# Layer 0 of a two-layer graph network on Trainium2: where a finished block's norm, flip and layer 1 products stand

## What is computed

```python
h = jnp.maximum(_layernorm(x), 0.0)
x = x + L0(h)   # feat = h @ W[type]; e = leaky_relu(el + er); softmax of e over the edges
                # of one target; sum over them of alpha * feat[src]; + h_bias
h = jnp.maximum(_layernorm(x), 0.0)
x = x + L1(h)   # h_all = h @ (8 relation matrices); sum over edges of h_all[src, type];
                # + h @ loop_w + h_bias + h; gelu; layer norm with gamma, beta
```

## Time and profile before

| | us |
|---|---|
| median of 3 runs | 2796.43 (2791.49 to 2800.01) |
| profiled execution, its span | 3432.1 |
| of it: until the first softmax (L1370) | 267.9 |
| the loop, first to last L1370 | 1673.9 |
| last L1370 to the first gather of layer 1 | 92.2 |
| first to last gather of layer 1 | 1361.7 |
| behind it | 36.4 |
| busy in the span: PE 1960.6, DVE 1538.5, ACT 667.0, POOL 2024.5 | |

### The profile page before, as it was taken

One profiled execution on the slowest core, in us unless ns is written; L12 is line 12 of the kernel. 1 busy time (PEld: TensorE's weight loads), 2 busy tenths in 40 slices (PEclk: granted clock), 3 DMA queues, 4 the chain that ended last, 5 costly groups with the idle time before them and its releaser, 6 DMA issues.

```text
span 3432.1 us, 26416 instructions
## 1 busy us (share of the span) xinstructions
PE 1960.6 (57%) x8092; PEld 1402.3 (41%) x8092; DVE 1538.5 (45%) x3220; ACT 667.0 (19%) x1202; POOL 2024.5 (59%) x2138
## 2 busy tenths in 40 slices
PE   7873536666665666566575772544544434554445
PEld 6772324444443444344453441333333322333334
DVE  6763546555655555455565540222332322323324
ACT  4423122333332323233323120000000000000001
POOL 6736555655555555555655527666666666666663
PEclk9985667788787878787787895666666766666667
DMA  8455334444443444444443333233333333333332
GB/s 229 158 189 174 103 98 119 128 132 130 131 136 111 138 122 128 120 129 120 135 133 112 97 129 104 84 93 93 98 98 92 97 92 100 96 95 98 97 92 70
DMA packets 168505, 403.12 MB, mean 117 GB/s; under 512 B 49741, under 2 KB 75820, under 8 KB 160682
## 3 DMA queue, kind: packets, MB, share of 16 engines
q0 software_dynamic: 95312, 261.58, 28.1%
q1 hardware_dynamic: 73050, 139.85, 11.8%
HBM read 325.41 MB, written 75.86 MB: 117 GB/s over the span
## 4 chain that ended last, share of the span: by engine, by line
PE 36%; another core or an unknown queue 28%; DVE 19%; issue 13%; ACT 1%; DVEq 1%; POOL 1%; DMA 0%; ACTq 0%; POOLq 0%
PE PB L1844 20%; PE PB L1955 6%; DVE ACC L1328 5%; DVE Z L1356 5%; PE PB L1796 4%; PE PB L1919 3%; DVE OHZ L1538 2%; DVE ERM L1337 1%; DVE OHZ L1346 1%; PE PB L1960 1%; POOL Z L841 1%; PE PB L1903 1%; DVEq L1315 0%; PE PB L1958 0%
## 5 line engine op out<-in xcount | busy, mean ns | idle before, releaser
L841 POOL DMA_INDIRECT Z<-tab,KI x1963 | 1868.2, 952 | 1260.0 <-issue 560.2
L1844 PE MATMUL PB<-Z,OHZ 128*128 128x260 f32 (+1 forms) x3926 | 1190.0, 459 | 808.0 <-issue 522.9
L1844 PEld LDWEIGHTS PB<-Z,OHZ 128*128 128x128 f32 x3926 | 861.5, 229 | 1085.3 <-issue 668.6
L1328 DVE TENSOR_TENSOR ACC<-ACC,PB 128x260 f32 (+1 forms) x997 | 421.4, 423 | 1493.4 <-remote 1031.1
L1919 PE MATMUL PB<-pick,ERM 128*128 128x16 f32 (+1 forms) x504 | 113.3, 375 | 476.2 <-DVE ERM L1337 440.4
L1919 PEld LDWEIGHTS PB<-pick,ERM 128*128 128x128 f32 (+1 forms) x504 | 109.9, 330 | 489.9 <-DVE ERM L1337 452.8
L1356 DVE TENSOR_TENSOR Z<-Z,PB 128x2048 f32<-128x2048 f32 (+1 forms) x125 | 283.9, 2271 | 0.0
L1955 PE MATMUL PB<-w,ht 128*128 128x512 f32 x480 | 271.5, 729 | 1.8 <-ACT ht L1714 1.8
L1776 ACT ACTIVATE ACC<-ACC 128x256 f32<-128x256 f32 x30 | 10.4, 406 | 857.2 <-DVE ACC L1328 857.2
L1955 PEld LDWEIGHTS PB<-w,ht 128*128 128x128 f32 x480 | 112.2, 241 | 139.0 <-issue 136.4
L1796 PE MATMUL PB<-wh,hx 128*128 128x424 f32 (+1 forms) x500 | 152.2, 375 | 20.7 <-DVE hx L933 15.7
(11 more groups left out here) (333 smaller groups left out, 1498.4 us busy)
## 6 DMA issues: line engine op xcount, KB each, us to landing
OHZ<-dlt SPq DMA_DIRECT2D x31, 1024.0 KB
Z<-tab,KI POOLq DMA_INDIRECT x1963
tab<-st SPq DMA_DIRECT2D x120, 256.0 KB
tab<-Z SPq DMA_DIRECT2D x24, 1040.0 KB, 4.3
TD<-typ SPq DMA_DIRECT2D x31, 256.0 KB
tab<-Z SPq DMA_DIRECT2D x5, 1024.0 KB, 8.1
xn<-xb SPq DMA_DIRECT2D x30, 128.0 KB
X<-xn SPq DMA_DIRECT2D x6, 640.0 KB
```

The source lines that it names most:

```text
L841: pool.indirect_dma_start(to, None, tab, at).then_inc(d_fe[g % 2][part(g, k) * layer], 16)
L1328: dv.tensor_tensor(a, a, bank(done + i)[:, 0:width], ALU.add).wait_op(*previous, "sem-ge").then_inc(*o.of(s_add))
L1844: last = pe.matmul(p, OH[:, slot, k + i, :], rows_, start=(i == 0), stop=(i == n - 1))
```

## The change

- `finish(r)` becomes a generator in two parts. Up to `ve` it runs behind `rescale` of its group, ahead of the second `scale_rows`; `rs` and `nmr` follow behind the adds of the first three pairs.
- On PE flip, products and own product of block r stand in group r+4, between the fourth pair and `select`. The quarters go to PB0, PB6, PB7 and PB1, the own product to PB0, the flip to PB1, each with a wait for the add that frees it (`s_add`). The fifth pair waits for `s_own`.
- On ACT `normed` and `move_flipped` stand behind the two exponentials of the group; the moves of the quarters and the own product stand behind `turned` and ahead of `stage` of the next turn.
- SP stores the block's table rows in the same group.
- After the loop the block in hand (27) is flipped in the midst of the last pairs, blocks 28 and 29 have a tile of their own each for the flipped rows (`HTL`), the transposes of the index tables stand between the products, and the three own products follow all quarters. The cast of `KI` is DVE's.

PE at the end of a group in the middle of the loop, before: from the first half of the next group's scores (L1903) to the softmax's transpose (L1986).

The core of the diff (PE's part and the sync engine's are told above and by the rows):

```diff
@@ finish(r) on DVE
-                norm_scale(r, r + 1, FIN + r)
+                dv.tensor_scalar(ve[:, r:r + 1], mv[:, r:r + 1, 1], 1e-5, None, ALU.add).then_inc(*o.of(s_ve))
+                yield
+                dv.wait_ge(s_sd, no)
+                dv.reciprocal(rs[:, r:r + 1], sd[:, r:r + 1]).then_inc(*o.of())
...
+                norm = finish(finished_in(g)) if finished_in(g) >= 0 else iter(())
+                next(norm, None)
                 for c in range(8, n, 8):
                     scale_rows(g, c)
...
+                    if c == 8:
+                        next(norm, None)
...
-                if finished_in(g) >= 0:
-                    finish(finished_in(g))
...
+            for i in range(2):
+                dv.wait_ge(s_pt, KT + i + 1)
+                dv.tensor_copy(KI[:, 512 * i:512 * i + 512], PB[6 + i][:, :]).then_inc(*o.of(s_ki))
@@ ACT's loop
                 if g + 1 < NG:
                     turned(g + 1)
+                r = finished_in(g - 1)
+                if r >= 0:
+                    for j in range(4):
+                        move_quarter(r, j)
+                    move_own(r)
+                if g + 1 < NG:
                     stage(g + 1)
...
                 ac.activation(EX[0:R, :], ZR[0:R, :], ACT.Exp).then_inc(*o.of(s_xr))
+                r = finished_in(g)
+                if r >= 0:
+                    normed(r)
+                    move_flipped(r)
@@ PE, flip and products
+                if r < LATE:
+                    pe.wait_ge(s_add, pair_no(r + 4, 1))
+                elif r > LATE:
                     pe.wait_ge(s_ev, moved(r - 1, 3))
...
+                    if r < LATE and j < 3:
+                        pe.wait_ge(s_add, pair_no(r + 4, j + 2))
...
+            block_products(LATE)
+            flip_block(LATE + 1)
             pe.wait_ge(s_loc, 4)
-            pe.wait_ge(s_own, last)
...
             pe.wait_ge(s_add, NPAIR)
+            turn_back(lambda t: ERM[:, 128 * t:128 * t + 128], (PB[6], PB[7]))
+            block_products(LATE + 1)
+            flip_block(LATE + 2)
+            turn_back(lambda t: TD[:, t, :], (PB[0], PB[1]))
+            block_products(LATE + 2)
+            for r in range(LATE, NB):
+                own_product_of(r)
```

More of the change, by code:

```diff
@@ L721, in _ @@
                 sp.dma_start(rows[:, i, :], t.rearrange("(o n) -> o n", o=1).to_broadcast([128, D])).then_inc(d_rows, 16)
[L722 to L730, removed]
+            store_block(LATE)
+            load_block(LATE + 2)
+            store_block(LATE + 1)
+            store_table(LATE)
+            store_block(LATE + 2)
+            store_table(LATE + 1)
+            store_table(LATE + 2)
             for i in range(2):
@@ L1457, in finish @@
                 s = r % 2
+                no = FIN + r
                 a = ACC[:, ROW0 * r:ROW0 * r + D].rearrange("p (h d) -> p h d", h=4)
@@ L1526, in _ @@
                     load_places(g + 1)
-                if finished_in(g) >= 0:
-                    finish(finished_in(g))
             for q in range(added_in_turn(NG - 1), GROUPS[NG - 1][1] // 2):
                 add(pair_no(NG - 1, q), ROW0, 0)
-            finish(NB - 2)
-            finish(NB - 1)
+            for r in range(LATE + 1, NB):
+                for _ in finish(r):
+                    pass
+            for i in range(2):
+                dv.wait_ge(s_pt, KT + i + 1)
+                dv.tensor_copy(KI[:, 512 * i:512 * i + 512], PB[6 + i][:, :]).then_inc(*o.of(s_ki))
             def onehot(g):
@@ L1695, in move_quarter @@
                     ac.wait_ge(d_st[j], 16 * r)
[L1696 removed]
+                ac.activation(ST1[:, j, :], quarter_bank(r, j)[:, :], ACT.Copy).then_inc(*o.of(s_ev))
             def move_own(r):
[L1700 to L1701 removed]
+                ac.wait_ge(s_mm, own_product(r))
+                ac.activation(ACC[:, ROW0 * r:ROW0 * r + D], own_bank(r)[:, 0:D], ACT.Copy).then_inc(*o.of(s_own))
             def normed(r):
@@ L1923, in late @@
             def late(g, a, b):
+                r = finished_in(g) if g >= 0 else -1
+                if a == 4 and 0 <= r < LATE:
+                    pe.wait_ge(s_own, r + 1)
                 for q in range(a, min(b, GROUPS[g][1] // 2)) if g >= 0 else ():
@@ L2007, in _ @@
                 late(g, 3, 4)
+                r = finished_in(g)
+                if 0 <= r < LATE:
+                    flip_block(r)
+                    block_products(r)
+                    own_product_of(r)
                 if g + 1 < NG:
                     select(g + 1)
[L2010 to L2031 removed]
+            late(NG - 1, 4, 8)
+            flip_block(LATE)
+            late(NG - 1, 8, 16)
+            block_products(LATE)
+            flip_block(LATE + 1)
+            pe.wait_ge(s_loc, 4)
+            pe.wait_ge(s_add, NPAIR)
+            turn_back(lambda t: ERM[:, 128 * t:128 * t + 128], (PB[6], PB[7]))
[3 more added lines that the diff above has]
+            block_products(LATE + 2)
+            for r in range(LATE, NB):
+                own_product_of(r)
+            pe.wait_ge(s_ki, 2)
+            pe.wait_ge(s_kt, KT + 2)
             pe.wait_ge(s_own, NB)
[L2033 removed]
             for g in range(len(GROUPS1)):
```

129 lines of the change are left out of this document (51 added, 78 removed).

## The result

| | us |
|---|---|
| before, median of 7 runs | 2796.43 (2791.49 to 2800.01) |
| after, median of 7 runs | 2808.54 (2801.67 to 2809.48) |
| ratio | 1.0039, 95% interval 1.0029 to 1.0049 |
| profiled execution of after, its span | 2807.0 |

The change makes the kernel 12 us slower; 33 us faster was forecast. The span of this record is that of the runs, so recording costs nothing here. The record of before came from an execution of 3432 us. The first set of experiments shows that the same kernel can take that long without a profile too; why it does stays open. All rows of "before" in this part are of that second record.

A forecast was written before the change was run, and what follows sets the result against it. The prediction took a chain of waits through DVE and PE to bound each group, with POOL second. Gains of 22 us in the loop and 11 behind it made 33: 2796.4 - 33 = 2763 us, range 2731 to 2804.

The forecast's parts named there:

- The two make 710, near the 636: Recorded span against median: late semaphores (560 us) and longer layer 1 gathers (150) were laid to recording, explaining 635.7 us.
- So the chain goes from 39.4 to 38.7: DVE and PE's scan-to-scan chain in the loop: 38.5 to 38.7 us, gain 0.8 a group, 22 us in 27 groups.
- POOL holds the group: Rival, chance 0.22: POOL's 32 gathers hold a group at 40.1 us, only the tail is won, 2785 us.
- the 0.30 between gathers may be the record's: POOL's gathers: the argument against POOL as bound, that the 0.30 us between gathers may come from recording.
- The middle of the group: Scan to `nmr` 20.7 us, then products 9.4 and own product 2.2 ahead of `select`; EV to scan 1.2.
- The clock: PE's moved products: 7.1 us at the high clock, 9.4 as recorded, 14.0 all at the low 1.2 GHz clock.
- Behind `select` only the way from EV to the scan is left: End of the group: about 1.2 us remain there, 12.1 us less between `select` and the scan.
- (37.5 + 42.5) / 2 = 40.0: POOL's fetch loop: scan to `select` end 37.5 us, `select` over the fetch to scan 42.5, alternating; POOL's own time 40.1.
- nothing is late: SP's queue: quarters stored at 30.4 to about 38 us, next masks issued at 46, so no delay.
- the ninth gather: POOL in the loop: its wait at this gather should go, while its wait for `select` grows from 9.5 towards 17 us.
- The tail: Behind the loop, last EV to layer 1's first gather: 11 us gained, between 4.9 and 13.5.
- The slower rival: Chance 0.17: low-clock products of over 10.5 us in the loop and a late next fetch; likely 2820 us, up to 2890.

The follow-up runs named there:

- The first set of experiments: Runs on a chip where the kernel before took a median of 3490 us: before unchanged (3482.7), altered POOL waits in both kernels, later table stores in after.
- that second record: The kernel before, unchanged, profiled again on the chip that ran most of the experiments: span 2793.3 us, measured 2795.0.
- warm: Kernel after plus eight matmuls with unused result behind `select`, filling PE's idle time ahead of the softmax's transpose: 2789.3 us, ratio to before 0.9958.
- gate_after_2: Kernel after, but a group's first gather waits for the fourth pair of two groups before, not for `select`: 2820.0 us, ratio to before 1.0078; an edit slip costs 15.
- store_next_2: Kernel after, but a block's table rows are stored one group later, ahead of the next block's sums: 2790.8 us, ratio to before 0.9976.
- mid_next: Kernel after with `select` between the second and third quarter of products and table rows stored one group later: 2788.0 us, ratio to before 0.9951.
- select_mid: Kernel after, but `select` stands between the second and third quarter of the block's products: 2790.2 us, ratio to before 0.9971.
- mid_next_warm: Kernel after with `select` between product quarters, table rows stored one group later, and eight extra matmuls behind the own product: 2788.7 us, ratio to before 0.9957.

## Why the prediction was wrong, step by step

- **"The two make 710, near the 636": wrong.** The late semaphores and the longer gathers were laid to recording. The records of before and after at 2793 and 2807 us show neither, and the runs at 3490 us without a profile are as long as with one. It was right that the timed kernel doesn't have the 14 us waits, so the model of a group without them was usable. The same reasoning also shortened the gathers of layer 1, which is right at 1.25.
- **"So the chain goes from 39.4 to 38.7", 22 us: the step that failed first.** The size of the chain was right: EV to the end of `select` and on to the next scan is 38.5 in after (38.7 forecast), and before PE had 0.7 us to spare in a group of 40.1 (39.4 forecast). But the chain was not what bounds the group. The group before was at 40.11 with POOL never waiting, so nothing on PE or DVE could shorten it. This was the rival "POOL holds the group". The text set it aside since "the 0.30 between gathers may be the record's"; the rows above show it in the undisturbed record as well. Its own estimate of the group without the late semaphores, 38.7, was "about POOL's own time", which leaves no room for a gain. With that case the forecast would have been 2785, still on the wrong side.
- **The middle of the group: right in its parts.** The products took 9.47 (9.4 forecast) and own product 2.2, EV to the scan 1.34 (1.2). From scan to the end of `nmr` it was 22.3 on average instead of 20.7. The 1.6 are the late pairs at the lower clock; in `warm`, with the late pairs at full clock, it is 20.6.
- **The clock: watched at the wrong place.** The text asked whether the products would run at 1.2 GHz, and gave the slower case to them. They were no slower. Taking the products away from the end of the group opened an idle time in front of the transpose, and the clock fell for the pairs behind it (1.94 us for four matmuls instead of 1.05). "Behind `select` only the way from EV to the scan is left" counts what is no longer on that path, and not what PE does there instead: nothing, for 3 us.
- **POOL: the right loop with a wrong term.** "(37.5 + 42.5) / 2 = 40.0" is (37.2 + 44.5) / 2 = 40.9 in the rows, counted from the scan as there. The first term held, since what the low clock cost, `select` gave back: it runs at the upper level now, 1.86 us instead of 3.6. The second term is 2.0 too small, 1.6 of it the landing, the rest the start of the fetch behind `select` (0.3) and the scan. Landing was taken as 2.4, from a stretch without table stores. It was 3.3 before, and in the new place, where four stores go out within 2.7 us right ahead of the last gather, it is 4.0. The text looked at SP's queue for lateness ("nothing is late") and not at what its transfers run beside. And the ninth gather, whose wait was said to go, closes a second loop of nearly the same length.
- **The tail: right, 8.0 instead of 11**, inside the 4.9 to 13.5 of the prediction. Its length goes with the clock in the first 8 us behind the last EV, in all seven kernels that have the whole change: 68.3 at 0.58 (after), 65.7 to 66.0 at 0.79 (`gate_after_2`, `store_next_2`, `mid_next`), and 64.4 at 1.00 (`select_mid`, `warm`, `mid_next_warm`), which is a gain of 11.9. After, `mid_next`, `select_mid`:

```profile
1512.60:1520.60 8.00, 7.21 (x21) 5.60 (x22) 5.29 (x23) 0.20 (x1) 6.17 (x7) 0.58 0.23 57
```

```profile
1495.50:1503.50 8.00, 7.23 (x29) 5.77 (x29) 5.79 (x24) 0.20 (x1) 6.17 (x7) 0.79 0.21 57
```

```profile
1498.80:1506.80 8.00, 7.30 (x36) 6.06 (x37) 7.07 (x27) 1.04 (x2) 6.07 (x7) 1.00 0.27 65
```

- **The slower rival** ended on the right side (2820) and named the late start of the next fetch, which is what the trace shows. Its cause (products of 10.5 us or more) was not the one.

What is shown: less landing time (`store_next_2`), a full clock (`warm`) or an earlier `select` (`select_mid`) each takes back 14 to 16 of the loop's 20 us, and 2 to 4 more in the tail. None acts on one term alone: in `warm` landing falls too, and in `select_mid` the late pairs are shorter. An earlier permission for POOL alone (`gate_after_2`) takes back nothing in the loop. What stays open: how the 20 us divide between landing, clock and the place of `select`; why the gathers of the changed order take 4 ns more each; and what delays the semaphores on the chip with 3490 us, where the changed kernel itself was not timed.

## What to carry to other kernels

Ask first whether some engine issues without a gap; if one does, a shorter chain elsewhere is worth nothing, and a longer one costs as soon as it closes a loop back to that engine. When work is moved off the end of a stage, look at the engine that it leaves: an idle time ahead of the next burst can cost the clock, and that may be dearer than the work was. Note for each moved transfer what it will run beside, and not only whether its queue is late.

## What the runs showed of the hardware

- Eight matmuls of 128x256 more in each of 27 groups (3.70 us of PE in the group shown) made the kernel 19 us faster. In after 2.6 to 5.1 us of idle time ahead of the transpose were followed by a granted clock of 0.50 (1.2 GHz) for the next 5 us, in all 25 groups; after 0.37 us (before) and 0.93 us (`warm`) it was 1.00 (2.4 GHz). The idle time alone does not fix it: in `select_mid` 3.58 us were followed by 0.68, and in `store_next_2` both 4.83 and 1.97 us by about 0.68. The Trainium skill (TensorE: Matmul & The Clock Gate, Why this matters for your kernels) asks to keep the array busy between bursts; these runs agree, and put a price on it here.
- A landing of gathered rows (start of the last gather to the first instruction that reads them) was 2.8 us with no table stores beside it, 3.3 where 1 MB of stores was issued from 3.8 us ahead of the last gather to 2.0 behind it, and 4.0 where all of it was issued from 3.7 to 1.0 us ahead. The DMA engines' busy share behind the last gather was 0.40, 0.74 and 0.97.
- Indirect gathers in a row took 1.25 to 1.26 us each, 0.95 of work and 0.30 between them, in every kernel on the faster chip. Together they are the floor of a group, 40.1 to 40.3 us, though POOL's busy share there is 0.76, below the 0.83 of PE. On the slower one layer 1's gathers were 1.41 to 1.42 apart.
- Two chips ran the same program in 2797 and 3490 us. On the slower one adds waited 1010 to 1354 us in all for releases without a maker near them. The record of such an execution misled the prediction about where a group spends its time.
